# A running sum in a state-space stage: from accumulating transfers to adds on the GpSimd engine

## The reference

```
dA  = exp(delta[..., None] * A)                 # 512 channels x 16 states per token
dBu = delta[..., None] * u[..., None] * Bm[:, :, None, :]
h_t = dA_t * h_(t-1) + dBu_t
y_t = sum over the 16 states n of h_t[:, n] * C_t[n]
out = ((y + u * D) * silu(res)) @ W_out
```

## Time and profile before

| | us |
|---|---|
| three runs | 3331.57, 3332.95, 3336.9 |
| median | 3332.95 |
| the profiled execution, its own time | 3336.9 |
| its span | 3335.1 |

### The profile page before, as it was taken

The page is one execution under the profiler, slowest core; times in us unless marked ns, Lnnn a source line. Parts: engine busy times, 40 slices in busy tenths (PEclk is TensorE's granted clock), DMA queues, the critical chain, the costliest instruction groups (busy, mean ns, idle before and its releaser), DMA issues.

```text
span 3335.1 us, 40739 instructions
## 1 busy us (share of the span) xinstructions
PE 2797.5 (84%) x13719; PEld 1686.9 (51%) x13782; DVE 2184.5 (65%) x3943; ACT 1569.1 (47%) x2311; POOL 1043.2 (31%) x705
## 2 busy tenths in 40 slices
PE   7778887787764699999966999948988887999999
PEld 3444454454452355555543666624444444666666
DVE  0698898899893676777532222226777775777776
ACT  2677667766761245555541111137777782111111
POOL 0887787788871111112102111012111100010000
PEclk9898998999866899999988999978999998999999
DMA  3354444454552744555323000010000002000000
GB/s 108 80 112 107 105 104 103 96 113 103 111 110 61 105 70 83 86 89 95 63 104 81 26 23 23 17 49 13 7 7 7 7 1 58 7 7 13 7 7 13
DMA packets 120347, 198.60 MB, mean 60 GB/s; under 512 B 15728, under 2 KB 78064, under 8 KB 118992
## 3 DMA queue, kind: packets, MB, share of 16 engines
q1 hardware_dynamic: 97504, 124.24, 16.5%
q0 software_dynamic: 22640, 71.75, 10.9%
HBM read 107.12 MB, written 25.91 MB: 40 GB/s over the span
## 4 chain that ended last, share of the span: by engine, by line
PE 51%; ACT 5%; DVE 5%; issue 4%; DMA 2%; POOL 0%; SPq 0%; ACTq 0%; DVEq 0%; POOLq 0%
PE PS L1517 7%; PE PS L2222 7%; PE PS L2240 6%; PE PS L1539 4%; PE PS L1810 3%; PE PS L1182 2%; PE PS L1859 2%; ACT Z L1963 2%; PE PS L1817 2%; PE PS L1161 2%; PE PS L1164 2%; PE PS L1109 1%; PE PS L1139 1%; PE PS L1877 1%; PE PS L1208 1%
## 5 line engine op out<-in xcount | busy, mean ns | idle before, releaser
L702 POOL TENSOR_TENSOR Z<-Z 128x1024 f32<-128x1024 f32 x256 | 652.7, 2661 | 109.5 <-PE PS L472 109.3
L652 DVE TENSOR_TENSOR_SCAN Z<-PS,Z 128x1024 f32<-128x1024 f32 x256 | 583.3, 2279 | 7.7 <-ACT PS L584 7.7
L472 PE MATMUL PS<-Z 128*128 128x128 f32 x2048 | 313.9, 301 | 139.8 <-DVE Z L665 131.9
L472 PEld LDWEIGHTS PS<-Z 128*128 128x128 f32 x2048 | 259.1, 156 | 288.4 <-DVE Z L652 145.2
L584 ACT ACTIVATE PS<-Z 128x511 f32<-128x511 f32 x512 | 332.2, 683 | 91.9 <-DVE Z L652 91.0
L1275 ACT ACTIVATE Z<-PS 128x512 f32<-128x512 f32 x320 | 189.1, 597 | 262.5 <-PE PS L1164 259.0
L2222 PE MATMUL PS<-Z 128*128 128x512 f32 x576 | 273.8, 600 | 17.5 <-DVE Z L2355 17.5
L440 PE MATMUL PS<-Z 128*128 128x512 f32 x512 | 254.6, 614 | 36.3 <-ACT Z L519 35.6
L2273 ACT ACTIVATE Z<-PS 128x512 f32<-128x512 f32 x144 | 86.0, 597 | 416.8 <-PE PS L2222 416.8
L1370 DVE TENSOR_REDUCE Z<-PS 128x1 f32<-128x512 f32 (+2 forms) x384 | 182.7, 508 | 114.6 <-PE PS L1140 109.9
L1963 ACT ACTIVATE Z<-Z 128x2048 f32<-128x2048 f32 x128 | 252.7, 2000 | 10.3 <-PE PS L1859 8.5
(11 more groups left out here) (278 smaller groups left out, 5021.6 us busy)
## 6 DMA issues: line engine op xcount, KB each, us to landing
Z<-Z POOLq DMA_DIRECT2D x120, 512.0 KB, 4.6
Z<-rows_b SPq DMA_DIRECT2D x128, 256.0 KB, 3.1
Z<-scr SPq DMA_DIRECT2D x256, 128.0 KB, 5.7
scr<-Z SPq DMA_DIRECT2D x32, 384.0 KB
Z<-in_L_ffn_expert_wv SPq DMA_DIRECT2D x4, 2048.0 KB, 14.6
rows_y<-Z SPq DMA_DIRECT2D x35, 128.0 KB, 1.7
Z<-in_L_attn_x SPq DMA_DIRECT2D x8, 512.0 KB, 8.9
rows_n<-Z SPq DMA_DIRECT2D x8, 512.0 KB, 2.9
```

What stands on the lines that cost most here:

```text
L472: ins = e.transpose(o[:, c * 128:(c + 1) * 128], self.h(k, c // 2)[:, c % 2, i * 128:(i + 1) * 128], ident)
L652: e.tensor_tensor_scan(h, a, h, 0.0, ALU.mult, ALU.add).then_inc(s["scan"], 1)
L702: e.tensor_tensor(self.h(k, f), self.du[b % 2][:, 2 * f:2 * f + 2, :], b3(self.Bs[k % 2], 1, [128, 2, 512]), ALU.mult).then_inc(s["hin"], 1)
```

## The change

The accumulating transfer of add(k) becomes one instruction of POOL, in place, over the same 128x1024 values. Its semaphore counts 1 for each add where the transfer counted 16, so the three places that wait for it change their numbers. Nothing moves in the order, no buffer changes, and the other stages are untouched. There are 15 adds in each of 8 batches, 120 in all.

```diff
@@ pe, back(b, c)
-                e.wait_ge(s["yadd"], 16 * 15 * (b + 1))
+                e.wait_ge(s["yadd"], 15 * (b + 1))
@@ act, turn(k, f)
-                    e.wait_ge(s["yadd"], 16 * (15 * b + n - 2 if n >= 2 else 15 * b))
+                    e.wait_ge(s["yadd"], 15 * b + n - 2 if n >= 2 else 15 * b)
@@ pool, add(k)
             e.wait_ge(s["yprod"], 2 * k + 2)
             if n > 1:
-                e.wait_ge(s["yadd"], 16 * (15 * b + n - 1))
+                e.wait_ge(s["yadd"], 15 * b + n - 1)
             o = self.acc[b % 2][:, 2:4, :]
-            e.dma_start(o, self.pr[k % 2], accum_op=ALU.add).then_inc(s["yadd"], 16)
+            e.tensor_tensor(o, o, self.pr[k % 2], ALU.add).then_inc(s["yadd"], 1)
```

## The result

| | us |
|---|---|
| changed kernel, median of four runs | 3357.27 (3347.2 to 3364.81) |
| kernel before, median of four runs on the same chip | 3334.74 (3331.57 to 3336.9) |
| ratio, with its 95% interval | 1.0067 [1.0044, 1.0091] |
| profiled execution of the changed kernel, span | 3359.76, 3358.0 |

The kernel is 22.5 us slower, where I forecast 8.8. The sign is right and the time lies in the range, but the size is short by more than half. So the question is where the other 14 us are.

The account below looks back on a forecast made before the run. DVE was taken to set StageA's pace, with POOL nearly full after the change. Terms of 4.4 (batch 0 to 1), 3.0 (middle) and 1.4 (last batch) gave +8.8 us on the median 3332.95, so 3342 us, range 3331 to 3366.

Parts of the forecast that it names:

- The price of an add: On POOL, an add takes 2.313 us from start to start, like the fills in a row.
- All POOL work together: From StageA's first fill to its last, fills, adds and du need 889.6 of 893.0 us, so POOL just keeps pace.
- Batch 0 to 1: First change of batch: POOL falls behind, du starts at 190.4 for 186.53, the scan of n = 3 is late: +4.4 us.
- A wait that changes place: DVE's L635 and clip wait out a running POOL operation: 0 in the sum, -1.4 to +2.3 us for each of six batches.
- The middle periods: du 1 to du 7: the add of n = 13 ends 0.5 us late in each of six periods, +3.0 us.
- The last batch: End of StageA: the scan of unit 127 is 4.3 us late, part is given back, PE's back starts +1.4 us.
- The sum: Whole kernel: 4.4 + 3.0 + 1.4 = +8.8 us, everything behind StageA shifting at cost 0.
- Rival 1: POOL becomes the bound throughout, clip's lock and the gates at silu and PE eating its spare time: about 3355, chance 0.23.
- Rival 2: Faster: ACT's wait for the transfer's landing was on the path and goes, 13 us, to 3320; chance 0.12.
- Rival 3: Nothing to be seen: POOL's lead over the scans absorbs all but the ends, +1.4 to +4.4 us, about 3336; chance 0.20.

Follow-up runs that it names:

- Experiment 5: Changed kernel with L635 as four one-input instructions and clip moved from DVE to POOL, ahead of du: 3412.07 us, ratio 1.0241.
- experiment 4: Changed kernel with each add over 128x512 values in place of 128x1024, leaving out half of ACT's sum: 3328.62 us, ratio 0.9990.
- experiment 12: Changed kernel with L635 as four one-input instructions and clip also writing a running sum (clipped values not the reference's): 3342.14 us, ratio 1.0042.
- experiment 3: Changed kernel with each add moved half a unit earlier in POOL's order, before a fill in place of behind it: 3355.37 us, ratio 1.0070.
- experiment 8: Changed kernel with adds on POOL only for n up to 10 and transfers for n > 10: 3349.54 us, ratio 1.0053.
- experiment 9: The changed kernel run again without any edit: 3359.06 us, ratio 1.0071.
- experiment 1: Changed kernel with L635 rewritten as four instructions of one tensor input each: 3358.85 us, ratio 1.0086.
- experiment 10: Changed kernel with L635 as four one-input instructions and clip cut into rows of odd length: 3354.45 us, ratio 1.0060.
- experiment 11: Changed kernel with L635 as four one-input instructions, clip cut into odd rows and adds half a unit earlier: 3362.99 us, ratio 1.0090.
- experiment 2: Kernel before with L635 rewritten as four instructions of one tensor input each: 3332.69 us, ratio 1.0005.
- experiment 7: Kernel before with the accumulating transfer issued half a unit earlier: 3334.35 us, ratio 1.0000.
- experiment 6: Changed kernel with L635 as four one-input instructions, clip on POOL and adds half a unit earlier: 3392.32 us, ratio 1.0188.

## Why it came out so, step by step

**The price of an add: right.** From start to start it takes 2.31 us (123.33 to 125.64 in batch 0), its mean is 2381 ns, and the fills fell to 2384.

**All POOL work together: right.** It nearly fills the time from batch 0 on (2.6 to 5.9 us idle in the two middle periods shown). Experiment 5 shows that further work comes through nearly in full, experiment 4 that half an add per unit costs nothing.

**Batch 0 to 1: the queue right, the lock missed.** I counted 27 operations from the fill at 127.92 to du. That run of operations is there, unbroken, but starts at 130.60, since PE releases its first fill 2.7 us later than before; 130.60 + 27 x 2.313 = 193.05, and in experiment 12 du starts at 193.06. So without the lock du is 6.5 us late, where I had 3.9. The changed kernel adds the lock's 7.0 us: du at 200.04.

**The step that failed is "A wait that changes place".** It took the lock at 0 and bounded it by 2.3 us a batch, because the only row of it lasted one POOL operation. I read that length as the mechanism: wait out the operation that runs. The Trainium skill (SBUF — State Buffer, "Who interferes with whom") has the rule of the exclusive pair of ports, and the traces agree with it so far: with one tensor input of one element each (0.58 us) nothing waits. Its wait until the other's instruction finishes is too short for batch 0, where the measurement decides: 10.91, 11.30 and 10.90 us over four seams each (the changed kernel, experiments 3 and 8). In the middle batches the same instruction is let in at the next seam (0.92 us). What differs in the traces is how far POOL is behind: it ran unbroken from 130.60 to 193.1 in batch 0, while at 541.22 it still stood for PE. Clip at the last change of batch fits this (2.78 us 10 us behind a pause of POOL, 5.97 us 20 us behind one, experiment 9), but that it decides was not tried. I had the fact that POOL would never be idle, and did not ask how an instruction gets in between operations that follow each other without a pause.

**Why undoing L635 alone brought nothing: shown in part.** The wait moved to clip, which has to be over before du, so du still waits for POOL's run to end and then for clip. Only with both locks away (experiment 12) did the time fall, from 3357 to 3359 us to 3342; by ratio from 1.0067 and 1.0071 to 1.0042, whose intervals overlap. Against experiment 1 (1.0086 [1.0068, 1.0103]), from which it differs in the form of clip alone, the intervals stand apart. In the traces StageA ends 18.1 us sooner than in the changed kernel: 7.0 us of it lie before du of batch 1, 11.9 in the middle, and 0.8 are given back at the end.

**The middle periods: +3.0 forecast, +11.3 measured.** The mechanism that I gave (the late add of n = 13) doesn't show as what costs: halving ACT's waits gained nothing in experiment 3, and in experiment 12, which keeps the order and has all adds on POOL, the middle was no longer than before. In the changed kernel PE's busy time for the same matmuls carries it, at 0.90 granted in three of the six periods; in the pair compared above it is lost 67 to 106 us behind du, where the clock falls. Stalls of DVE at clip don't explain that clock: in experiment 3 clip takes 2.4 us or more in each of these changes of batch and no period is at 0.90, and in experiment 4 one is, with clip at 1.21. What remains is a count, from one profile each: periods at 0.90 or less are three in both profiles of the changed kernel, four in experiments 1 and 10, one each in 4, 8 and 11, and none in the kernel before (where one of 118.6 us stands at 0.92) and in experiments 2, 3, 7 and 12 (experiments 5 and 6, whose periods are longer anyway, left aside). Why the changed kernel meets the low clock more often stays open, and so does whether the other values that clip writes in experiment 12 have a part in it; the kernel before was not run with that form of clip.

**The last batch: +1.4 forecast, +1.4 measured.** The part that is given back at the end is there: the last add (2.34 us, 1038.23 to 1040.57) is followed by PE's back at 1040.67, as worked out.

**The sum.** Without locks StageA ends 8.1 us late, for 8.8 forecast. That is partly luck: the terms were 6.5, -0.6 and 2.1 in place of 4.4, 3.0 and 1.4. By medians experiment 12 is 0.0042 x 3328.5 = 14 us slower [9 to 19], so 8.8 lies at the edge. For the whole loss an estimate can be made from the clock of all executions: its mean is 0.922 in 27 of the changed kernel and 0.925 in 66 of the kernel before, and in both the time falls by 2.3 to 3.5 us for each 0.001. So 5 to 8 us go with the lower clock, and 18 to 20 remain at an equal one, near the 8.1 of the queue and the 7.0 of the lock in batch 0.

**The rivals.** Rival 1 named the right time (3355) and two causes, "clip's lock and the gates". Clip's lock is 1.2 us a batch in the middle and didn't fill POOL: it has idle time in every middle period, and the mark that I set (du to du of 119 or more) turned out to be one of PE's clock: experiment 4 reaches 119.35 us with POOL idle for 21.9. An add of 2.66 us did not occur. Rival 2 (faster) is refuted by the result itself, and experiments 3 and 7 show no gain from halving ACT's waits. Rival 3 is refuted by the ratio of the changed kernel, and by 1.0042 of experiment 12.

No version was faster than the kernel before: experiments 2, 4 and 7 equal it, and experiment 4 leaves out work.

## What to carry to other kernels

Before work is moved to POOL, add up its queue against the stretch: at 890 of 893 us there is no room, and a wait of another engine that was hidden before can then cost, as L635 did. List the DVE instructions that contend with POOL for the port, and ask for each when POOL next has a pause; if that pause itself waits for DVE (as du for clip), the instruction stands until POOL's queue has run dry. And compare PE's busy time for the same count of matmuls before a longer period is put down to the engine that was changed.

## What the hardware showed that I had not expected

- A DVE instruction of 0.16 us was passed over at four seams of POOL's operations: 10.91 us.
- It is mutual: where clip was let in at a seam (it started at 902.75 and lasted 2.78 us), the POOL fill that starts at 904.40 took 3.32 us instead of 2.36.
- Clip as max and min in one instruction takes 7073 ns on POOL, more than du's two-input product of the same size (4530 ns), and 1.21 us on DVE.
- Clip with a running sum takes 2.28 us on DVE, beside a busy POOL or not, where the plain form takes 1.21 alone and up to 5.97 beside it (experiment 9).
- Two equal stretches of one kernel differ by 3.3 us in 116, nearly all of it where the granted clock is low: the same 14 matmuls took 1.7 us longer at one place.
